# Batch norm at the end of a graph kernel: half of it folded into the turning product

## What is computed

```python
h = relu(layernorm(x))
agg = segment_sum(edge_weight * (h @ W)[col], row) + bias    # 625x256
mean, var = agg.mean(0), agg.var(0)                          # over the nodes
out = x + relu((agg - mean) * rsqrt(var + eps) * gamma + beta)
```

## Time and profile before

| what | us |
|---|---|
| median of 3 runs | 114.17 |
| lowest, highest | 113.99, 114.22 |
| profiled execution | 114.17 |
| its span, first to last instruction | 112.4 |
| TensorE (PE) busy | 100.6, 89% of the span |
| VectorE (DVE) busy | 92.5, 82% |
| ScalarE (ACT) busy | 57.4, 51% |
| GpSimd (POOL) busy | 19.8, 18% |

### The profile page before, as it was taken

How to read it: one execution, slowest core, us unless ns; L and a number is a source line. 1 busy time by engine, 2 the same in 40 slices (tenths; PEclk the granted TensorE clock), 3 DMA queues, 4 the chain that set the end, 5 groups by cost and what they waited for, 6 DMA issues and landing times.

```text
span 112.4 us, 2688 instructions
## 1 busy us (share of the span) xinstructions
PE 100.6 (89%) x1040; PEld 92.4 (82%) x1040; DVE 92.5 (82%) x266; ACT 57.4 (51%) x143; POOL 19.8 (18%) x27
## 2 busy tenths in 40 slices
PE   0398999799999999999899999998999998999930
PEld 0335898687998899989899999997999997999720
DVE  2399999999999999999986699767989989437950
ACT  2497999997897690312807035506233145141630
POOL 7100000000000099410093700660000000000000
PEclk9999999999999999999999999999999999999997
DMA  1867810000200000000153000000000000000044
GB/s 42 239 207 181 281 34 0 0 6 3 92 7 0 6 9 6 0 0 3 14 172 99 0 0 0 0 6 0 0 6 0 0 0 0 0 0 6 0 109 121
DMA packets 5401, 4.63 MB, mean 41 GB/s; under 512 B 555, under 2 KB 5386, under 8 KB 5386
## 3 DMA queue, kind: packets, MB, share of 16 engines
q1 hardware_dynamic: 4460, 3.68, 11.5%
q10 hardware_dynamic: 926, 0.75, 2.4%
HBM read 3.79 MB, written 0.64 MB: 39 GB/s over the span
## 4 chain that ended last, share of the span: by engine, by line
PE 36%; issue 24%; DVE 21%; ACT 7%; POOL 5%; DMA 3%; DVEq 0%; SPq 0%; POOLq 0%; ACTq 0%
PE bank L1125 8%; PE bank L1127 7%; PE bank L1126 7%; PE bank L1375 7%; DMA edge_rows_i<-in_dst_dram 3%; DVE stats L534 3%; DVE pre L741 3%; DVE x_in L674 2%; POOL parts L480 2%; POOL own L489 2%; PE bank L1415 2%; PE bank L1188 2%; DVE h_lo L751 2%; DVE pre L745 1%; PE bank L1275 1%
## 5 line engine op out<-in xcount | busy, mean ns | idle before, releaser
L581 DVE TENSOR_SCALAR src_hot<-node_id,edge_cols 125x626 f16<-125x626 f16 x77 | 23.5, 380 | 0.0
L1275 PEld LDWEIGHTS bank<-dst_hot,src_hot 125*128 125x128 f16 x505 | 19.0, 98 | 3.3 <-DVE src_hot L581 1.7
L1275 PE MATMUL bank<-dst_hot,src_hot 125*128 125x84 f16 (+6 forms) x505 | 20.4, 195 | 1.4 <-DVE src_hot L581 0.9
L1375 PE MATMUL bank<-counts,u_lo 125*128 125x312 f32 (+1 forms) x60 | 16.3, 308 | 0.0
L1051 ACT ACTIVATE h_hi<-pre 128x312 fp32r<-128x312 f32 (+1 forms) x12 | 5.6, 466 | 18.1 <-DVE pre L745 18.1
L480 POOL TENSOR_TENSOR parts<-parts 125x625 f32<-125x625 f32 x5 | 6.4, 1297 | 43.1 <-DVE src_hot L581 35.9
L1375 PE MATMUL bank<-counts,u_hi 125*128 125x312 f32 (+1 forms) x48 | 14.0, 307 | 0.0
L1375 PEld LDWEIGHTS bank<-counts,u_lo 125*128 125x128 f32 x60 | 10.9, 189 | 0.0
L994 ACT ACTIVATE parts<-bank 125x250 f32<-125x250 f32 x25 | 10.2, 411 | 0.0
L1375 PEld LDWEIGHTS bank<-counts,u_hi 125*128 125x128 f32 x48 | 9.1, 189 | 0.0
L918 ACT ACTIVATE counts<-bank 125x125 fp32r<-125x125 f32 (+1 forms) x25 | 7.4, 297 | 2.0 <-PE bank L1275 2.0
(11 more groups left out here) (143 smaller groups left out, 252.8 us busy)
## 6 DMA issues: line engine op xcount, KB each, us to landing
raw<-in_L_gnn_W_dram SPq DMA_DIRECT2D x3, 512.0 KB, 6.5
x_in<-in_x_dram ACTq DMA_DIRECT2D x1, 560.0 KB
raw<-in_L_gnn_Wf_dram SPq DMA_DIRECT2D x1, 512.0 KB, 3.8
out_dram<-x_in SPq DMA_DIRECT2D x2, 168.0 KB
wf<-in_L_gnn_Wf_dram SPq DMA_DIRECT2D x1, 256.0 KB, 7.8
raw<-in_L_gnn_Wf_dram SPq DMA_DIRECT2D x1, 256.0 KB, 2.8
raw<-in_L_gnn_W_dram SPq DMA_DIRECT2D x1, 256.0 KB, 3.5
out_dram<-x_in SPq DMA_DIRECT2D x2, 112.0 KB
```

The costliest lines, as they stand in the source:

```text
L581: dve.tensor_scalar(src_hot[:, t % RING, 0:IDS], node_id[:, 0:IDS], edge_cols[:, 0, t:t + 1], None, ALU.is_equal).then_inc(src_hot_vector, 1)
L1275: return pe.matmul(built[s][:, :, n0:n0 + n], src_hot[:, t % RING, BLK * s:BLK * s + P], dst_hot[:, c, :, j // 2, c0:c0 + n, j % 2], start ...
L1375: ins = pe.matmul(bank[KF * h + f][:, 0:e - a], u[:, k, P * f:P * (f + 1)], counts[0:BLK, k, a:e], start=False, stop=(k == NB - 1 and u is ...
```

## The change

- The four groups are cut anew: g2 is (f=1, blocks 0,1,2), g3 is (f=1, blocks 3,4).
- VectorE: three tiles are new. `ones` is set at the start. `shift_diag` is the identity times beta of f = 1, made behind `s_low`. `scale_diag` is the identity times gamma/std of f = 1.
- VectorE's order: the statistics of (1,0) are taken before the reciprocal of f = 0. For f = 1, `shift` is only the negated mean of the product, and (1,0) is centred by an addition. The reciprocal and the diagonal follow behind that.
- ScalarE: (1,1) is centred with `Identity` and a bias, ahead of copy_out(0), with no wait for the scale.
- TensorE: put_x(0) stands behind the four products. `put_shift` opens the banks of g2 and g3 with ones times the diagonal of beta. The turns of g2 and g3 are products with the diagonal of scale, added to the bank. Relu and the adding of x (`add_rows`) are as before.

```diff
+        scale_diag = sb("scale_diag", [P, P], F32)
+        shift_diag = sb("shift_diag", [P, P], F32)
+        ones = sb("ones", [P, BLK], F32)
...
-        Y_GROUPS = [[(f, b) for b in blocks] for f in range(KF) for blocks in ((0, 1), (2, 3, 4))]
+        Y_GROUPS = [[(0, 0), (0, 1)], [(0, 2), (0, 3), (0, 4)], [(1, 0), (1, 1), (1, 2)], [(1, 3), (1, 4)]]
...
+            dve.memset(ones[:, :], 1.0)
...
-            for f in range(KF):
-                for h in range(2):
-                    moments_of_agg(f, h)
-                variance_of_agg(f)
-                centre(f)
-                affine(f)
-            dve.wait_ge(bn_ready, 2)
-            dve.wait_ge(scale_ready, 2)
+            dve.tensor_scalar(shift_diag[:, :], ident[:, :], vec(5, 1), None, ALU.mult).then_inc(shift_diag_ready, 1)
+            moments_of_agg(0, 0)
+            moments_of_agg(0, 1)
+            variance_of_agg(0)
...
+            moments_of_agg(1, 0)
+            dve.wait_ge(std_ready, stds[0])
+            step.add(dve.reciprocal(rstd[:, 0:1], rstd[:, 0:1]))
...
+            moments_of_agg(1, 1)
+            variance_of_agg(1)
+            dve.scalar_tensor_tensor(out=shift[:, 1:2], in0=vec(3, 1), scalar=moments[:, 1, 0:1], in1=vec(3, 1),
+                                     op0=ALU.subtract, op1=ALU.subtract).then_inc(mean_ready, 1)
+            dve.wait_ge(mean_ready, 1)
             a, e = HALVES[0]
-            dve.tensor_scalar(pre_t[:, 1, a:e], groups.bank[("agg", AGG.index((1, 0)))][:, 0:e - a], scale[:, 1:2],
-                              shift[:, 1:2], ALU.mult, ALU.add).then_inc(y_ready_vector, 1)
+            dve.tensor_scalar(pre_t[:, 1, a:e], groups.bank[("agg", AGG.index((1, 0)))][:, 0:e - a], shift[:, 1:2],
+                              None, ALU.add).then_inc(centred_vector, 1)
+            dve.wait_ge(std_ready, stds[0])
+            step.add(dve.reciprocal(rstd[:, 1:2], rstd[:, 1:2]))
+            step.wait()
+            dve.tensor_scalar(scale_diag[:, :], ident[:, :], rstd[:, 1:2], vec(4, 1), ALU.mult,
+                              ALU.mult).then_inc(scale_diag_ready, 1)
...
             root(rstd[:, 1:2], moments[:, 1, 1:2])
+            act.wait_ge(mean_ready, 1)
+            a, e = HALVES[1]
+            nc.scalar.activation(pre_t[:, 1, a:NODES], groups.bank[("agg", AGG.index((1, 1)))][:, 0:NODES - a],
+                                 ACT.Identity, bias=shift[:, 1:2]).then_inc(centred, 1)
             copy_out(0)
-            act.wait_ge(scale_ready, 2)
-            act.wait_ge(bn_ready, 2)
-            affine(1, 1)
             copy_out(1)
...
-            put_x(0)
             pe.wait_ge(*LO_W4)
...
+            def put_shift(i):
+                n = len(Y_GROUPS[i])
+                pe.wait_ge(shift_diag_ready, 1)
+                pe.matmul(fill(("y", i))[0:BLK, 0:P * n], ones[:, :], shift_diag[:, :].unsqueeze(1).to_broadcast([P, n, P]),
+                          start=True, stop=False, skip_group_check=True)
+            def turn_rows(i):
+                o = groups.bank[("y", i)]
+                for n, (f, b) in enumerate(Y_GROUPS[i]):
+                    if f:
+                        pe.wait_ge(scale_diag_ready, 1)
+                        if b <= 2:
+                            pe.wait_ge(centred_vector, 1)
+                        if b >= 2:
+                            pe.wait_ge(centred, 1)
+                    else:
+                        pe.wait_ge(y_ready, 1 if b < 2 else 2)
+                    ins = pe.matmul(o[0:BLK, P * n:P * (n + 1)], pre_t[:, f, BLK * b:BLK * (b + 1)],
+                                    (scale_diag if f else ident)[:, :], start=False, stop=(n == len(Y_GROUPS[i]) - 1),
+                                    skip_group_check=True)
+                ins.then_inc(filled, 1)
+            put_x(0)
             put_x(1)
-            for i, pairs in enumerate(Y_GROUPS):
...
-                    if f:
-                        ins = pe.transpose(to, rows, ident[:, :])
...
+            put_shift(2)
+            turn_rows(0)
+            put_shift(3)
+            turn_rows(1)
+            turn_rows(2)
+            turn_rows(3)
```

More of the change, by code:

```diff
@@ L352, in gnn_kernel @@
         y_ready = sem("y_ready")
-        y_ready_vector = sem("y_ready_vector")
+        mean_ready = sem("mean_ready")
+        centred = sem("centred")
+        centred_vector = sem("centred_vector")
+        scale_diag_ready = sem("scale_diag_ready")
+        shift_diag_ready = sem("shift_diag_ready")
         out_ready = sem("out_ready")
@@ L870, in variance_of_agg @@
                             stats[:, 2 * f:2 * f + 2, :].rearrange("p a b -> p (a b)")).then_inc(variance_ready, 1)
-            def centre(f):
                 dve.wait_ge(variance_ready, stds[0])
[L874 to L886, removed]
             def add_rows(i):
@@ new lines, in _ @@
+            moments_of_agg(0, 0)
+            moments_of_agg(0, 1)
+            variance_of_agg(0)
+            step.add(dve.scalar_tensor_tensor(out=shift[:, 0:1], in0=moments[:, 0, 0:1], scalar=vec(3, 0),
+                                              in1=vec(3, 0), op0=ALU.add, op1=ALU.subtract))
+            step.wait()
+            step.add(dve.scalar_tensor_tensor(out=shift[:, 0:1], in0=shift[:, 0:1], scalar=-1.0,
+                                              in1=vec(4, 0), op0=ALU.mult, op1=ALU.mult))
@@ new lines, in _ @@
+            moments_of_agg(1, 0)
+            dve.wait_ge(std_ready, stds[0])
+            step.add(dve.reciprocal(rstd[:, 0:1], rstd[:, 0:1]))
+            step.wait()
+            dve.tensor_tensor(scale[:, 0:1], rstd[:, 0:1], vec(4, 0), ALU.mult).then_inc(scale_ready, 1)
+            dve.scalar_tensor_tensor(out=shift[:, 0:1], in0=shift[:, 0:1], scalar=rstd[:, 0:1],
+                                     in1=vec(5, 0), op0=ALU.mult, op1=ALU.add).then_inc(bn_ready, 1)
+            moments_of_agg(1, 1)
@@ L1462, in _ @@
                 ins.then_inc(filled, 1)
-            put_x(1)
-            for i, pairs in enumerate(Y_GROUPS):
-                o = fill(("y", i)) if i >= 2 else groups.bank[("y", i)]
-                for n, (f, b) in enumerate(pairs):
-                    to, rows = o[0:BLK, P * n:P * (n + 1)], pre_t[:, f, BLK * b:BLK * (b + 1)]
-                    if f:
[L1469 to L1472, removed]
-                        ins = pe.transpose(to, rows, ident[:, :])
[L1474 to L1477, removed]
+            def put_shift(i):
[19 more added lines that the diff above has]
+            put_x(0)
+            put_x(1)
+            put_shift(2)
[4 more added lines that the diff above has]
+            turn_rows(3)
 _INS = ['x', 'src', 'dst', 'edge_weight', 'L0_gnn_W0', 'L0_gnn_b0', 'L0_gnn_W1', 'L0_gnn_b1', 'L0_gnn_W2', 'L0_gnn_b2',
```

## The result

The changed kernel takes 114.72 us (median of 5 runs, 114.65 to 114.79), the kernel before, in its runs beside it, 113.99 (113.55 to 114.22). The ratio is 1.0063, 95% interval 1.0046 to 1.0080: **slower by 0.6%**. The profiled executions are 114.73 and 114.17 us, the spans 112.9 and 112.4.

What follows compares the result with a forecast made beforehand. The prediction took the stream of stores from g1 on as setting the end: TensorE's added queue makes g1's store 0.85 us later, less 0.10 for a denser stream, +0.75 on 114.17, so 114.9 us, range 114.45 to 115.2.

Steps and rivals of the forecast that it cites:

- TensorE's queue: TensorE behind the last products: puts and turns up to g1's last sum to 3.28 us, making g1's store 0.85 us later.
- Two records by the diagonal, not four: Turns of g2 and g3: each diagonal product takes two 0.11 us records; four would make g3's store 1.1 us later still.
- rival 3: TensorE: a product with a broadcast or diagonal operand runs in one record; end at +0.2, 114.35; chance 0.04.
- The removal of put_x(0) from its old place: Ahead of TensorE's last products: shortens the first of them, moving everything behind 0.06 us earlier, bounds nothing to 0.08.
- Issues: SyncE's stores of g1, g2 and g3 are issued at 108.79, 109.51 and 109.84 us.
- Costs of nothing: VectorE's statistics order, shift_diag, ones and the diagonal (0.25 us, ready 107.15) are covered by waits or TensorE's puts: no cost.
- from the issues to the end: Final stores: g1's 0.85 us delay moves the end, less 0.10 us for a denser stream (at most 0.28): +0.75.
- Rival 1: Final stores: the last transfer alone decides, g3 not queueing behind g1 and g2; end at +0.25, 114.4; chance 0.12.
- Rival 2: VectorE's path to the diagonal (107.15) stays the bound; g3's store 0.2 us earlier, at most 0.28 faster, 113.9; chance 0.05.

Runs made afterwards that it cites:

- thinning of the puts of beta: Changed kernel with ones and beta's diagonal in the rounded 32-bit type, one record per put instead of two; 1.0019 against the kernel before.
- the three edits: Changed kernel with put_x(0) back ahead of the last products, one-record puts of beta straight behind put_x(1), VectorE's old order; 0.9997 against the kernel before.
- the last three kernels: The three edits (0.9997); those with g2's and g3's turns by the identity (0.9965); those with ScalarE centring both halves, VectorE copying g1 (0.9975).
- ScalarE and VectorE swapped: The three edits, plus ScalarE centring both last-feature halves while VectorE makes the diagonal first and copies g1; 113.69 us, 0.9975 against the kernel before.

## Why the prediction was right

Right: the sign, the cause and the order of size. 114.9 was said, 114.72 measured; against the runs of before beside it that is +0.73 us (0.53 to 0.91 by the interval), between the two profiled executions +0.56, where the sum had +0.75. The 0.18 us by which the absolute number is off is the base: the sum stood on 114.17, and before's median beside the changed kernel was 113.99. That +0.75 and +0.73 are so close is in part luck, as two terms below show.

- **TensorE's queue.** 3.28 us of records were summed from the rows; from the first put at 104.89 to g1's last record at 108.03 and its 0.11 it is 3.25. The thinning of the puts of beta and the move of put_x(0) gave back their records in the issues (0.74 of 0.79 us, 0.44 of 0.44); the removal of the puts of beta gave back 0.67 to 0.79 of 1.09, the rest turned, by its trace, into waits for ScalarE.
- **Two records by the diagonal, not four.** 0.11 us each, two per turn: ten for the five blocks, where the transposing turns of the kernel before have five. The puts of beta show two records each as well, so rival 3 is refuted.
- **The removal of put_x(0) from its old place** was to give 0.06 us and gave none. The first product's row reads 0.38 us again, and it waits for VectorE's low half of s:

```profile
101.34 0.38 PE L1137 MATMUL bank<-s_hi,w_hi 128*128 128x312 f32 x1 [0.26 <-DVE s_lo L831]
```

  The lower bound, nothing, was the truth. The excess of 0.07 over an ordinary row is there without the put ahead of it, so it was not the put's. Nor do the other profiles show a gain: the last product starts between 104.56 and 104.96 where put_x(0) stands ahead, between 104.63 and 105.09 where it stands behind.
- **Issues.** 108.79, 109.51 and 109.84 were said, 108.86, 109.58 and 109.95 came: late by 0.07 us, which is mostly these 0.06, and the last by 0.04 more.
- **Costs of nothing.** The order of the statistics is confirmed by a run. The diagonal took 0.35 us, not 0.25, and stood at 107.31 instead of 107.15, 0.8 us ahead of its use.
- **The step that was sized worst: from the issues to the end.** I took 0.10 us off the 0.85 by which g1 is late, with 0.28 as the bound. Between the two profiles g1 is 0.92 late and the release 0.55: 0.37 came off, more than the bound. From g1's issue to the release before took 4.07 us, against a floor of 3.66; part of that is the middle (218 against 242 GB/s), part the thin tail (0.7 us at 66 GB/s, now 0.5 at 39). But about half of these 0.41 us is the one profile: with the same issues, put_x(0) late in the kernel before took 3.86 us, at 232 GB/s. Against it only 0.16 came off (0.90 less 0.74, counted from the last product), and the medians, +0.73, agree with that. So I took off 0.1 to 0.3 us too little; with one profile of each kernel it stays open where in between, and why the stream was thinner in the first profile. That g1 went 0.07 us later than the sum had it hid a part of this. (The other two above 4 us, the new cut alone with 4.05 and the three edits with 4.02, are held by g2, which they issue later behind g1.)
- **Rival 1** said +0.25, where +0.73 came, and its reason falls too: a lone store needs 1.96 us, not 2.61. The formula that the prediction sets beside it from the Trainium skill (DMA: Bandwidth & Descriptors, Anatomy of one DMA) is given there for transfers that GpSimd issues; by it a lone store of 128 KB would take 2.3 us, an estimate, and SyncE's took 1.96. **Rival 2**, VectorE's path, is what binds as soon as the backlog is gone, as the last three kernels show.

## What to carry to other kernels

Work added to an engine with idle time is free only up to the wait that it fills: the same put cost nothing in one kernel and about its full 0.44 us in the other. Before a path is shortened on one engine by giving work to another, add up the other's records between its last input and its next wait. And price an f32 product by its records: here two per matmul, one for the transposing or the rounded form.

For stores at the end, look at (issue + time for all bytes still to go) store by store and take the latest, not the first or the last issue alone. It is a fit to a few tenths of a us, and it missed the kernel before by 0.4.

## What the runs showed of the hardware beyond that

- A put of beta in the rounded 32-bit type has one record whose printed duration is longer than that of one of the two f32 records (628 against 486 ns at 384 columns), although TensorE gets through faster: with ScalarE and VectorE swapped, the chain gives both puts of beta 0.29 us together, where in the changed kernel they have 0.65 and 0.43. Durations reach to modelled ends; the distances of starts price a record.

```profile
105.62 0.29 PE bank L1479 x2
```

- A tensor_scalar with one per-partition operand took 0.54 us over 312 columns from a bank, with two 0.61; ScalarE's Identity with a bias took 0.52 over 313 columns where Relu with bias and scale took 0.61.
- In the changed kernel TensorE's granted clock stays at 1.00 (2.4 GHz) to the end of the stream, where it was 0.51 on average, the lower level of 1.2 GHz, from 111.0 on in the kernel before; TensorE's last record ends at 109.4 instead of 108.7. TensorE had no work there any more, so it cost nothing.
